# Attention scores from two twelve-bit float32r parts, two heads at a time in TensorE's row halves

## What is computed

```python
def _attn(q_in, k_in, v_in, wq, bq, wk, bk, wv, bv, wo, bo, causal):
    Q = (q_in @ wq + bq).reshape(Bq, Sq, H, HD)      # H = HD = 16
    Kp = (k_in @ wk + bk).reshape(Bq, Sk, H, HD)
    scores = jnp.einsum('bqhd,bkhd->bhqk', Q, Kp) / jnp.sqrt(jnp.float32(HD))
    if causal:
        scores = jnp.where(mask, scores, -jnp.inf)
    a = jax.nn.softmax(scores, axis=-1)
    ...
x = _layernorm(x + _attn(x, x, x, ..., True), ...)
x = _layernorm(x + _attn(x, encoder_output, encoder_output, ..., False), ...)
x = _layernorm(x + _moe(x, ...), ...)                # 8 experts, 2 per token, gelu
```

## Time and profile before

| | |
|---|---|
| median of 3 runs | 756.76 us (755.46, 756.76, 758.52) |
| profiled execution: span of the core | 755.9 us |
| median less that span | 0.8 us |
| TensorE busy | 711.2 us, 94% of the span |
| VectorE, ScalarE, GpSimd busy | 499.0, 369.2, 287.3 us |
| granted TensorE clock, mean | 0.983 of full speed |
| attention | from 28 us to about 500 us; from 420 us with experts between |

### The profile page before, as it was taken

How to read it: one execution, slowest core, us unless ns; L and a number is a source line. 1 busy time by engine, 2 the same in 40 slices (tenths; PEclk the granted TensorE clock), 3 DMA queues, 4 the chain that set the end, 5 groups by cost and what they waited for, 6 DMA issues and landing times.

```text
span 755.9 us, 14560 instructions
## 1 busy us (share of the span) xinstructions
PE 711.2 (94%) x4969; PEld 478.4 (63%) x4969; DVE 499.0 (66%) x1376; ACT 369.2 (49%) x749; POOL 287.3 (38%) x558
## 2 busy tenths in 40 slices
PE   6889999999999999999997889999999999999983
PEld 4444434545464454645563666898999999999941
DVE  5679788678766877756687744365666665666436
ACT  4325475665666676677753436433433332332403
POOL 8305521542653463624654333212332332232114
PEclk9999999999999999999997989999999999999997
DMA  8954431343164021316037762676999999999754
GB/s 273 291 145 128 114 98 46 84 129 128 34 179 127 13 60 48 92 43 179 14 113 237 223 210 95 204 262 226 357 328 343 343 326 341 343 332 333 236 187 163
DMA packets 95154, 140.29 MB, mean 186 GB/s; under 512 B 11855, under 2 KB 81077, under 8 KB 92597
## 3 DMA queue, kind: packets, MB, share of 16 engines
q1 hardware_dynamic: 76357, 107.86, 45.5%
q10 hardware_dynamic: 15072, 22.02, 9.1%
q0 software_dynamic: 3648, 9.45, 3.5%
HBM read 110.65 MB, written 28.65 MB: 184 GB/s over the span
## 4 chain that ended last, share of the span: by engine, by line
PE 75%; issue 8%; DVE 7%; DMA 5%; POOL 2%; ACT 1%; SPq 0%; DVEq 0%; ACTq 0%; POOLq 0%
PE out_acc L984 11%; PE score_pair L961 10%; PE work L932 9%; PE score_pair L855 8%; PE work L849 8%; PE work L906 6%; PE work L855 4%; PE score_pair L849 3%; PE work L1008 3%; DVE neg_part_max L1472 3%; PE work L918 2%; PE work L992 2%; PE work L935 2%; DMA arena<-parts_scratch 1%; PE out_acc L849 1%
## 5 line engine op out<-in xcount | busy, mean ns | idle before, releaser
L1472 DVE TENSOR_REDUCE neg_part_max<-work 128x1 f32<-128x512 f32 (+4 forms) x368 | 213.3, 625 | 70.4 <-PE work L935 35.9
L1244 ACT ACTIVATE arena<-score_pair 128x1024 f32<-128x1024 f32 (+2 forms) x224 | 178.9, 839 | 79.8 <-PE score_pair L961 78.9
L932 PE MATMUL work<-arena 96*128 96x77 bf16 (+4 forms) x640 | 118.5, 278 | 10.3 <-ACT arena L1207 2.7
L961 PE MATMUL score_pair<-arena 99*128 99x512 bf16 (+2 forms) x448 | 104.2, 337 | 4.0 <-DMA arena<-negmax_scratch 3.0
L984 PE MATMUL out_acc<-arena 128*32 128x512 f32 (+4 forms) x896 | 103.7, 517 | 2.6 <-DVE arena L1492 2.6
L1904 POOL DMA_INDIRECT chosen_scratch<-arena,scatter_rows x36 | 35.6, 989 | 176.5 <-DVE arena L1404 176.2
L855 PE MATMUL score_pair<-arena 128*128 128x256 f32 x432 | 97.6, 380 | 0.0
L932 PEld LDWEIGHTS work<-arena 96*128 96x128 bf16 x640 | 49.5, 99 | 74.5 <-issue 31.0
L1960 POOL TENSOR_SCALAR_AFFINE_SELECT arena<-arena 128x256 f32<-128x256 f32 x128 | 51.5, 410 | 117.9 <-ACT arena L1244 116.7
L1177 ACT ACTIVATE arena<-work,expert_b_cols 128x128 f32<-128x128 f32 x180 | 51.1, 369 | 77.3 <-PE work L849 64.0
L849 PE MATMUL work<-arena 128*128 128x128 f32 x720 | 87.7, 279 | 0.3 <-issue 0.3
(11 more groups left out here) (257 smaller groups left out, 955.0 us busy)
## 6 DMA issues: line engine op xcount, KB each, us to landing
arena<-in_L_xattn_e_w SPq DMA_DIRECT2D x54, 1024.0 KB, 7.1
arena<-parts_scratch SPq DMA_DIRECT2D x24, 768.0 KB, 6.1
arena<-in_L_xattn_e_w ACTq DMA_DIRECT2D x18, 1024.0 KB, 6.4
parts_scratch<-arena_more SPq DMA_DIRECT2D x24, 384.0 KB, 2.6
parts_scratch<-arena_more SPq DMA_DIRECT2D x24, 256.0 KB, 3.0
parts_scratch<-arena_more SPq DMA_DIRECT2D x24, 128.0 KB, 2.9
residual<-in_x SPq DMA_DIRECT2D x4, 512.0 KB, 8.1
tokens_scratch<-residual SPq DMA_DIRECT2D x2, 1024.0 KB, 5.4
```

The lines of the kernel that those rows point to most:

```text
L932: m = pe.matmul(bank[:, j * it.w:(j + 1) * it.w], qa[st.half(it.g)][0:R_S, h, n0:n0 + P], k, start=True, stop=not it.last)
L961: m = pe.matmul(st2[pair][0:rows, j, 0:w], k, qa[st.half(it.g)][0:R_M, h, skip:QG], start=True, stop=True)
L1244: act_e.activation(pt[buf][0:rows, :, 0:w], st2[pair][0:rows, :, 0:w], ACT.Exp, scale=float(HD) ** -0.5).then_inc(pair_taken[pair], 1)
L1472: dve.tensor_reduce(pm[:, it.at, it.t, it.h0:it.h0 + it.nh], bank[:, 0:it.nh * it.w].rearrange("p (j k) -> p j k", j=it.nh), AX.X, ALU.max ...
```

## The change

Queries and keys are split into two float32r parts of twelve bits each, instead of three bfloat16. Three products of parts are then wanted: 48 rows to a head, and 50 with the two parts of the maximum. They fit a half of the array's rows, so even heads lie on partitions 0 to 63 and odd heads on 64 to 127, and the two matmuls of a pair of heads follow each other, one in each half, with outputs in two PSUM banks.

- A step "max" now does two heads, takes two of the three `work` banks, and signals each; VectorE does two reductions behind it. There are 184 such steps instead of 368. The mask is added once for all heads of a bank, in two turns of 64 rows for each half.
- "score" pairs an even and an odd head.
- The split leaves out one part: in stages 0, 6 and 7 a ScalarE copy and a VectorE subtraction, elsewhere two of GpSimd's three operations. "gather" has two GpSimd operations instead of four, "lay" one float32 transpose instead of four bfloat16.
- A projection is stored by two DMAs instead of three, a load is two DMAs (one for each row half) instead of one, and so is that of the maxima; the bytes of stores and loads stay.
- The rows of ones are now set over whole buffers, and the SP queue waits for them before it loads keys. Buffers move so that `ka`, `qa` and `kac` have a tensor of their own, which the experts' weights use later.
- `ORDER` keeps its sequence but for the halved `m` and `n`.

```diff
-Q_PART = (0, 0, 0, 1, 1, 2)
-K_PART = (0, 1, 2, 0, 1, 0)
+Q_PART = (0, 0, 1)
+K_PART = (0, 1, 0)
...
-                    for j in range(it.nh):
-                        h = it.h0 + j
-                        k = kac[st.slot][0:R_S, h, 0:it.w] if st.cross else ka[st.slot][0:R_S, it.at, h, 0:it.w]
-                        m = pe.matmul(bank[:, j * it.w:(j + 1) * it.w], qa[st.half(it.g)][0:R_S, h, n0:n0 + P], k,
-                                      start=True, stop=not it.last)
-                        if it.last:
-                            m = pe.matmul(bank[:, (j + 1) * it.w - P:(j + 1) * it.w], identb[:, :], mask_qk[:, :],
-                                          start=False, stop=True)
-                    m.then_inc(full[it.bank], 1)
+                    for i in range(it.nh):
+                        h = it.h0 + i
+                        for j in range(2):
+                            rows = slice(j * ROWS, j * ROWS + R_S)
+                            k = kac[st.slot][rows, h, 0:it.w] if st.cross else ka[st.slot][rows, it.at, h, 0:it.w]
+                            done[j] = pe.matmul(banks[j][:, i * it.w:(i + 1) * it.w],
+                                                qa[st.half(it.g)][rows, h, n0:n0 + P].bitcast(f32r), k.bitcast(f32r),
+                                                start=(i == 0), stop=(i == it.nh - 1 and not it.last))
+                    for turn in range(2 if it.last else 0):
+                        for j in range(2):
+                            rows = slice(j * ROWS, (j + 1) * ROWS)
+                            to = banks[j][:, 0:it.nh * it.w].rearrange("p (h k) -> p h k", h=it.nh)[:, :, it.w - P:it.w]
+                            m = mask_qk[rows, turn, :].rearrange("p (o k) -> p o k", o=1)
+                            done[j] = pe.matmul(to, identb[rows, turn * ROWS:turn * ROWS + P],
+                                                bc(m, [ROWS, it.nh, P]), start=False, stop=(turn == 1))
+                    done[0].then_inc(full[it.bank], 1)
+                    done[1].then_inc(full[it.bank_b], 1)
...
                     for j in range(2):
-                        h = it.quad * QUAD + it.pair * 2 + j
+                        h, part = it.quad * 2 + it.pair, slice(j * ROWS, j * ROWS + R_M)
                         u, n0 = k0 // QG, k0 % QG
-                        k = kac[st.slot][0:R_M, h, 0:SE] if st.cross else ka[st.slot][0:R_M, u, h, n0:n0 + P]
-                        m = pe.matmul(st2[pair][0:rows, j, 0:w], k, qa[st.half(it.g)][0:R_M, h, skip:QG],
-                                      start=True, stop=True)
-                    m.then_inc(pair_full[pair], 1)
+                        k = kac[st.slot][part, h, 0:SE] if st.cross else ka[st.slot][part, u, h, n0:n0 + P]
+                        m = pe.matmul(st2[pair][0:rows, j, 0:w], k.bitcast(f32r),
+                                      qa[st.half(it.g)][part, h, skip:QG].bitcast(f32r), start=True, stop=True)
+                        m.then_inc(pair_full[pair], 1)
...
-                    dve.tensor_reduce(pm[:, it.at, it.t, it.h0:it.h0 + it.nh],
-                                      bank[:, 0:it.nh * it.w].rearrange("p (j k) -> p j k", j=it.nh),
-                                      AX.X, ALU.max, negate=True).then_inc(taken[it.bank], 1)
+                    for j, (i, use) in enumerate(((it.bank, it.use), (it.bank_b, it.use_b))):
+                        e.wait_ge(full[i], use)
+                        scores = work[i][:, 0:it.nh * it.w].rearrange("p (h k) -> p h k", h=it.nh)
+                        dve.tensor_reduce(pm[:, it.at, it.g, j, it.h0:it.h0 + it.nh, it.t % QT],
+                                          scores[:, :, 0:SE] if st.cross else scores,
+                                          AX.X, ALU.max, negate=True).then_inc(taken[i], 1)
...
-                    own.inc(pool.tensor_tensor(f, f, p[0], ALU.subtract))
-                    e.wait_ge(gstep, own.n)
-                    own.inc(pool.tensor_copy(p[1], f))
-                    e.wait_ge(gstep, own.n)
-                    pool.tensor_tensor(p[2], f, p[1], ALU.subtract).then_inc(third_g, 1)
+                    pool.tensor_tensor(p[1], p[1], p[0], ALU.subtract).then_inc(second_g, 1)
```

More of the change, by code:

```diff
@@ L39 @@
 R_S = NGR * HD
-R_M = R_S + 3
-TWO_ONES = float(np.array([0x3F803F80], np.uint32).view(np.float32)[0])
+R_M = R_S + 2
+ROWS = P // 2
+HALF = HH // 2
+SEW = SE + SE % 2
 NEG = -1e30
@@ L168, in maxima @@
         if st.cross:
-            steps += [Item("max", st=st, t=qb, g=u, w=SE, h0=h0, nh=HH // 2) for h0 in range(0, HH, HH // 2)]
+            steps.append(Item("max", st=st, t=qb, g=u, w=SEW, nh=HALF))
             continue
@@ L174, in maxima @@
             steps += [Item("max", st=st, t=qb, g=u, at=c, w=w, h0=h0, nh=BANK // w, last=(c + 1) * BANK >= keys)
-                      for h0 in range(0, HH, BANK // w)]
+                      for h0 in range(0, HALF, BANK // w)]
     return steps
@@ L346, in make_plan @@
             bank += 1
+        if it.kind == "max":
+            it.bank_b, it.use_b = bank % 3, bank // 3 + 1
+            bank += 1
     return plan
@@ L373, in build @@
 def build(nc, x, ctx_in, par, wts, router_w, w1, b1, w2, b2, out):
-    f32, bf16, i32, u32 = mybir.dt.float32, mybir.dt.bfloat16, mybir.dt.int32, mybir.dt.uint32
+    f32, f32r, bf16, i32, u32 = (mybir.dt.float32, mybir.dt.float32r, mybir.dt.bfloat16, mybir.dt.int32,
+                                 mybir.dt.uint32)
     ALU, ACT, AX = mybir.AluOpType, mybir.ActivationFunctionType, mybir.AxisListType
@@ L615, in build @@
             where = it.st.half(it.g)
-            so_far[where] = so_far.get(where, 0) + (16 if it.st.cross else 32)
+            so_far[where] = so_far.get(where, 0) + (32 if it.st.cross else 64)
             landed[it.st.n, it.g] = so_far[where]
@@ L742, in turn_read, with parts_ok, apart @@
             return (logit_sum, it.t % QT + 1) if it.kind == "r_mul_last" else (full[it.bank], it.use)
-        def third_ok(it):
-            return (third_v if it.st.in_a_hurry else third_g, third_of[it.n])
+        def parts_ok(it):
+            z = projected[it.st.n, it.at, it.g]
+            return (taken[z.bank], z.use) if it.st.in_a_hurry else (second_g, second_of[it.n])
+        def apart(parts, j):
+            return parts.rearrange("g (d h j) t -> j (g d) h t", h=HALF, j=2)[j]
         def heads_apart(to, landed_at):
@@ L937, in tensor @@
-                    m.then_inc(full[it.bank], 1)
+                    banks = bank, work[it.bank_b]
+                    done = [None, None]
+                    for i in range(it.nh):
[6 more added lines that the diff above has]
+                                                start=(i == 0), stop=(i == it.nh - 1 and not it.last))
```

210 lines of the change are left out of this document (101 added, 109 removed).

## The result

| | before | after |
|---|---|---|
| median of the runs | 757.34 us (755.46 to 758.52, 4 runs) | 842.1 us (840.67 to 845.63, 4 runs) |
| profiled execution: span | 755.9 us | 843.9 us |
| TensorE busy | 711.2 us, 94% | 750.8 us, 89% |
| TensorE not busy (span less busy) | 44.7 us | 93.1 us |
| granted TensorE clock, mean | 0.983 | 0.902 |

What follows compares the result with a forecast made beforehand. TensorE, ending last in self-attention, was taken as the bound. Gains of 4 + 26 + 2.5 + 0 + 1.5 = 34 us off the 755.9 us span gave 721.9, with 0.8 for the median 722.7, stated as 723 us; range 694 to 766 (0.80).

Steps and rivals of the forecast that it cites:

- Price of a pair: Scores and maxima: float32r at the bfloat16 rate, both halves at once, 0.216 us for 512 columns; gains 36.7 and 24.5 us.
- Narrow pairs: Pairs of 256 and of 128 columns: the weight load decides, 0.111 us each; about half as much if loads were fast.
- float32's rate: Rival for scores and maxima: a pair of 512 takes 0.432 us, kernel 18 us slower, 775 us; chance 0.11 including anything between.
- halves in turn: Rival for scores, maxima and mask: the two row halves do not run at once, 54 us slower, 811 us; chance 0.07.
- Change of shape: TensorE passing between half-row scores or maxima and whole-row work: 161 x 0.095 = 15.3 us of new cost.
- TensorE's own sum: All of TensorE's matmul work: 36.7 + 24.5 + 0.3 + 1.9 - 15.3 = 48 us less.
- What reaches the end: Share of TensorE's 48 us that shortens the run: 4, 26 and 2.5 us by window, 10 us lost to bank waits.
- swallowed: Rival in self-attention: two banks to one step leave VectorE and TensorE taking turns; 738 to 753 us, chance 0.15.
- Start: Up to the first maxima: a ScalarE copy and a subtraction go, net 1.5 us earlier, between 0 and 3.
- the mask: Mask matmuls of the maxima on TensorE: 14.6 us before, 14.3 after, no gain.
- the experts' stretch: The experts' part, from 500 us on: about 222 us, unchanged.

Runs made afterwards that it cites:

- the stream alone: TensorE alone, no waits, played the matmuls of the kernel before in written order, then those of the kernel after: 422.8 us and 394.5 us.

## Why the prediction was wrong

**Price of a pair: right.** 0.216 us forecast for 512 columns, 0.227 measured alone; two matmuls of a pair start 3 ns apart. In the kernel after, at the full clock, two pairs of scores and the pair of maxima behind them:

```profile
243.60 0.73 PE L990 MATMUL score_pair<-keys_queries 50*128 50x512 f32 x4
...
244.17 0.40 PE L957 MATMUL work<-keys_queries 48*128 48x512 f32 x2
```

By their single records the second pair starts 0.34 us after the first, and the third 0.24 after the second. The first pair stands behind a change of shape, and 0.10 of the 0.34 is what comes on top of one. Narrow pairs: 0.111 forecast, 0.11 measured for 78 columns and 0.12 for 256; the loads are not the cheap ones that the prediction left open. The rivals at float32's rate (775 us) and of halves in turn (811 us) are out, although the result lies beyond both.

**Change of shape: mis-sized by half.** 161 x 0.095 = 15.3 us stood in the sum, with 161 x 0.14 as the upper bound; measured 0.20 behind wide matmuls, so 32. The change itself was priced right, although the two readings at "weigh" were 0.09 and 0.14 and the choice of 0.095 was not worked out from them: 0.095 to 0.10 measured. The step that failed was to read the whole price off "weigh", whose weights are 32 columns wide, and to carry it to loads of 128 columns of four-byte weights, which delay the second matmul behind a change by 0.05 to 0.10 us more. The Trainium skill's "TensorEngine Tiling (Array Packing)", Key Properties, names the drain and no price; the measured 0.095 to 0.10 at the change itself bears the rule out. With 32 in place of 15.3, and 0.011 more for each of the 224 pairs of 512, TensorE's own sum is -48 + 17 + 2.5 = -28.5, and the stream alone came to -28. That this is so close is partly luck: the order of the kernel after has 154 such passages and not 161, narrow matmuls lose less than 0.20, and the loads behind "weigh", which the sum leaves out, lose some as well.

**What reaches the end: wrong, the coupling.** This is the first of the two steps that turned the sign. I charged 10 us for two of three banks and named the point from which it decides, a reduction pair (1.28 us) longer than the work between two steps. TensorE stood before maxima, waiting for a reduction, 72 times for 42.0 us. The rival called "swallowed" had the mechanism, at 20 us more and 743 us in all; in the kernel before the coupling costs 31 us by itself, and TensorE's time not busy rose by 48 in the kernel after. VectorE did not go from 74% to 86% between 76 and 342 us but to 66% (175.1 of 266 us): I had let a faster TensorE fill VectorE, as if one could run ahead of the other. With three banks and two to a step neither can.

**Clock: left out, the largest term.** This is the second. The prediction noted that the granted clock was full in the attention's windows and then used prices at full clock for a kernel with other shapes and more waits. It had no rival in which the level changes. That is 62 to 70 of the 116 us between TensorE's stream alone (-28) and the result (+88).

**Start: wrong sign.** Forecast 1.5 us earlier. The first "max" began at 32.95 us where it was 28.38 before. The setting of ones was "over before the parts have landed", which held, but it runs beside VectorE's copies: 2.91 and 3.60 us, 0.61 and 0.25 without it (2.64 and 0.71 in the kernel before). Taking it away gave 7 us in all and 2.5 at the first "max" (30.48). There the first store is issued at 13.86 us, 1.1 earlier than before (14.93), as forecast; but from the first load's issue to the first "max" 12.3 us pass (from 18.20), and 8.7 in the kernel before (from 19.67). "Below 1 us" for two DMAs in place of one was too little for this path, or something else on it takes longer; no run separates them.

**Right besides:** the mask gains nothing (14.3 us of 14.6 stay; left out, it gives back 11.5 us after and 9 before), and the experts' stretch is unchanged (219.64 of 222 us busy, 219.65 before).

## What to carry to other kernels

Sum a change of TensorE's work twice: as a stream played alone, which needs one small program, and as the waits that it meets, since a step that takes two of three buffers turns overlap into turns. A change that packs less of the array into each instant can lose its full clock where there are waits as well, as here; look at the granted clock of the stretch, put a rival with the lower level into the forecast (up to the length of the stretch once more), and charge every change between half-row and whole-row work 0.1 us, and up to 0.1 more where four-byte weights follow.

## What was not expected of the hardware

- One half of the rows alone (50 of 128 rows, 512 columns) took the granted clock from 1.00 to 0.50 while TensorE was never idle; both halves at once kept 1.00, and so did all 128 rows. Pairs of 78 columns took it to 0.50.
- float32r matmuls of 50 rows in both halves follow at 0.227 us for two of 512 columns; bfloat16 ones of 96 rows at 0.216 for one.
- A change between half-row and whole-row work delays the next matmul by 0.095 to 0.10 us; with four-byte weights the second one behind it comes another 0.05 to 0.10 us later, with bfloat16 ones 0.01.
- A VectorE copy of 8x128 float32 took 3.60 us beside a GpSimd memset of 128x4096 and 0.25 us without it; one of 128x512 took 2.91 and 0.61. Beside a memset of 3x4096, as long (3.51 us), the latter took 2.64.
